# DLRM tower on one core: third block's root and second layer ahead of the last transfers and linear layer, squares summed on VectorE, bias products over 128 columns

## The reference

```python
e = stack([tbl_n[ids[:, n]] for n in range(26)], axis=1)      # 512 x 26 x 64
x = layer_norm(r_dense_t @ Wd.T, gd, bd)                      # 512 x 128
y = layer_norm(einsum('bnd,ed->bne', e, Ws), gs, bs)          # 512 x 26 x 128
y = layer_norm(einsum('bne,pn->bep', y, Wsi), gsi, bsi)       # 512 x 128 x 32
T = concatenate([x[:, None, :], swapaxes(y, 1, 2)], axis=1)   # 512 x 33 x 128
Z = einsum('bnd,bmd->bnm', T, T)
z = layer_norm(Z[:, TRIL_I, TRIL_J] @ Wl.T, gl, bl)[:, :384]  # layer norm over 512
h = maximum(concatenate([z, r_dense_t], axis=1) @ W_top1 + b_top1, 0)   # 512 x 512
h = maximum(h @ W_top2 + b_top2, 0)                           # 512 x 256
return h @ W_top3
```

## Time and profile before

| | us |
|---|---|
| median of 3 runs | 175.03 (173.59 to 177.0) |
| profiled execution, its own time | 173.57 |
| its span, first to last instruction | 171.8 |
| mean granted clock of TensorE | 0.98 |
| busy: PE, PEld, DVE, ACT, POOL | 143.2, 108.4, 129.6, 99.4, 101.1 |
| gathers, line 257: 104 instructions | 99.7 busy, 958 ns each |
| idle between gathers | 31.4 |

### The profile page before, as it was taken

One profiled execution on the slowest core, in us unless ns is written; L12 is line 12 of the kernel. 1 busy time (PEld: TensorE's weight loads), 2 busy tenths in 40 slices (PEclk: granted clock), 3 DMA queues, 4 the chain that ended last, 5 costly groups with the idle time before them and its releaser, 6 DMA issues.

```text
span 171.8 us, 4668 instructions
## 1 busy us (share of the span) xinstructions
PE 143.2 (83%) x1825; PEld 108.4 (63%) x1825; DVE 129.6 (75%) x300; ACT 99.4 (58%) x245; POOL 101.1 (59%) x111
## 2 busy tenths in 40 slices
PE   0179878798989946599999998969998899996995
PEld 0075543545559534467878685849695776886994
DVE  6359777796989498859899996949999877943151
ACT  0302344779765788667798686736676846721330
POOL 3777777777777777777777777777777200020000
PEclk9999999999999699879999999999999999999999
DMA  4833616133111113311111231111112200010000
GB/s 154 271 90 96 257 23 213 28 87 91 29 31 27 30 23 69 63 27 31 25 34 29 59 69 27 31 27 31 27 30 64 54 8 18 23 41 0 0 0 0
DMA packets 6003, 9.59 MB, mean 56 GB/s; under 512 B 2303, under 2 KB 3538, under 8 KB 5854
## 3 DMA queue, kind: packets, MB, share of 16 engines
q0 software_dynamic: 3392, 3.45, 11.0%
q1 hardware_dynamic: 2232, 5.08, 9.5%
q10 hardware_dynamic: 358, 0.78, 1.2%
HBM read 8.01 MB, written 0.00 MB: 47 GB/s over the span
## 4 chain that ended last, share of the span: by engine, by line
POOL 48%; PE 22%; issue 17%; DVE 5%; ACT 3%; DMA 2%; ACTq 1%; DVEq 0%
POOL g_sb L257 48%; PE psB L320 3%; PE psW L354 3%; PE psH L374 2%; PE psG L286 2%; PE psZ L335 1%; DMA g_sb<-in_table,row_id 1%; PE psZ L426 1%; PE psU L301 1%; PE psW L399 1%; DMA ids_sb<-in_ids 1%; ACT U L602 1%; ACTq L214 1%; DVE ssB L842 1%; DVE B L835 1%
## 5 line engine op out<-in xcount | busy, mean ns | idle before, releaser
L257 POOL DMA_INDIRECT g_sb<-in_table,row_id x104 | 99.7, 958 | 31.7 <-issue 31.4
L835 DVE TENSOR_TENSOR B<-psB,bias 128x512 f32<-128x512 f32 x31 | 20.0, 687 | 17.0 <-PE psB L320 16.9
L301 PE MATMUL psU<-wsi_x,g_sb 128*128 128x192 f32 (+4 forms) x128 | 21.3, 311 | 6.5 <-DVE g_sb L828 6.5
L301 PEld LDWEIGHTS psU<-wsi_x,g_sb 128*128 128x128 f32 x128 | 19.3, 193 | 10.1 <-DVE g_sb L828 10.1
L613 ACT ACTIVATE sqB<-B 128x512 f32<-128x512 f32 x31 | 19.1, 632 | 10.7 <-DVE B L835 10.5
L641 ACT ACTIVATE Zs<-psZ 32x264 f32<-32x264 f32 x59 | 22.3, 378 | 1.6 <-PE psZ L335 0.6
L320 PE MATMUL psB<-U,ws_g 64*128 64x512 f32 x64 | 19.9, 701 | 3.4 <-ACT U L602 3.3
L855 DVE TENSOR_TENSOR T<-B,psG 128x512 f32<-128x512 f32 x31 | 21.3, 687 | 1.1
L286 PEld LDWEIGHTS psG<-gram,sT 128*128 128x128 f32 x104 | 13.3, 197 | 13.7 <-ACT sT L589 10.8
L842 DVE TENSOR_REDUCE ssB<-sqB 128x16 f32<-128x512 f32 x32 | 21.7, 678 | 0.1
L286 PE MATMUL psG<-gram,sT 128*128 128x128 f32 x104 | 16.3, 297 | 0.7 <-ACT sT L589 0.7
(11 more groups left out here) (160 smaller groups left out, 217.2 us busy)
## 6 DMA issues: line engine op xcount, KB each, us to landing
g_sb<-in_table,row_id POOLq DMA_INDIRECT x104, 2.5
wl_sb<-in_wl SPq DMA_DIRECT2D x1, 1280.0 KB, 5.9
w_sb<-in_w SPq DMA_DIRECT2D x2, 512.0 KB, 5.4
w_sb<-in_w SPq DMA_DIRECT2D x1, 768.0 KB, 4.2
small_sb<-in_small SPq DMA_DIRECT2D x1, 615.5 KB, 3.7
dense_sb<-in_dense ACTq DMA_DIRECT2D x1, 512.0 KB, 7.2
Zt<-Zs SPq DMA_DIRECT2D x3, 80.0 KB
Zt<-Zs SPq DMA_DIRECT2D x3, 70.0 KB
```

The source lines that it names most:

```text
L257: pool.indirect_dma_start(g_sb[:, k, h * DSP:(h + 1) * DSP], None, table, bass.IndirectOffsetOnAxis(row_id[:, 2 * k + h:2 * k + h + 1], 0) ...
L301: mm = pe.matmul(psU[:, (lo - US * j) * PROJ:(hi - US * j) * PROJ], g_sb[:, SLOTS * b + c, :], wsi_x[:, c, lo - s0:hi - s0, :], start=(n = ...
L835: dve.tensor_tensor(B[:, h, :].rearrange("p (s j) -> p s j", j=PROJ), psB[h][:, :].rearrange("p (s j) -> p s j", j=PROJ), bias[:, :].rearr ...
```

## The change

1. ScalarE behind the steps: the third block's root (`deviation_w(LAST - 1)`) stands ahead of the relays. ScalarE issues one relay (q = 1) and GpSimd three (q = 2, 4, 6).
2. TensorE: `third_layer2(2, K1)` stands in front of the wait for the relays and in front of the whole linear layer of the last block, no longer behind its first quarter.
3. Last block: VectorE adds the four squares by three additions, and TensorE makes one product with ones where it made four. `top1(LAST, 1)` stands ahead of it. ScalarE's ReLU of the third block's second layer stands behind the last square.
4. `bias_part` takes its twelve products with the bias column repeated over 128 columns, six in step 4 and six in step 5; VectorE takes every 128th column of the bank at step 6. `shift_part` is spread over steps 1, 2 and 3 (1, 2 and 2 products), and VectorE takes its result at step 4.

```diff
-            for q in (2, 6):
+            for q in (2, 4, 6):
                 relay(pool, LAST, q, 1, 2, d_zt_pool)
...
             def last_block():
+                third_layer2(2, K1)
                 pe.wait_ge(d_zt[LAST], 10 * 16)
-                pe.wait_ge(d_zt_act, 2 * 16)
-                pe.wait_ge(d_zt_pool, 2 * 16)
+                pe.wait_ge(d_zt_act, 16)
+                pe.wait_ge(d_zt_pool, 3 * 16)
...
                 last_linear(0)
-                third_layer2(2, K1)
                 last_linear(1)
...
                 top1(LAST, 0, psF[0][:, 0:BS])
+                top1(LAST, 1, psF[0][:, BS:2 * BS]).then_inc(h1_f, 1)
                 pe.wait_ge(W_sd, LAST)
-                for f in range(FLIN // P):
-                    pe.wait_ge(sq_f, f + 1)
-                    mm = pe.matmul(psV[:, 0:BS], ones_sb[:, :], z_sq[:, f * BS:(f + 1) * BS], start=(f == 0),
-                                   stop=(f == FLIN // P - 1))
-                mm.then_inc(W_summed, 1)
-                top1(LAST, 1, psF[0][:, BS:2 * BS]).then_inc(h1_f, 1)
+                pe.wait_ge(sq_added, 3)
+                pe.matmul(psV[:, 0:BS], ones_sb[:, :], z_sq[:, 0:BS], start=True, stop=True).then_inc(W_summed, 1)
...
-            def bias_part():
-                pe.wait_ge(d_w1, 16)
-                pe.wait_ge(x1_ready, 1)
-                for f in range(K1):
+            def bias_part(lo, hi):
+                if lo == 0:
+                    pe.wait_ge(d_w1, 16)
+                    pe.wait_ge(x1_ready, 1)
+                for f in range(lo, hi):
                     for k in range(KZ):
-                        mm = pe.matmul(psH[:, f:f + 1], w1_sb[:, k, f * P:(f + 1) * P], bl_c[:, k:k + 1],
-                                       start=(k == 0), stop=(k == KZ - 1))
-                mm.then_inc(bz_done, 1)
+                        mm = pe.matmul(psH[:, f * P:(f + 1) * P], w1_sb[:, k, f * P:(f + 1) * P],
+                                       bl_c[:, k:k + 1].broadcast_to([P, P]), start=(k == 0), stop=(k == KZ - 1))
+                if hi == K1:
+                    mm.then_inc(bz_done, 1)
...
             keep_z(UNITS - 1, 1)
+            deviation_w(LAST - 1)
             act.wait_ge(Z_kept, 4 * UNITS)
-            for q in (1, 4):
-                relay(act, LAST, q, 1, 2, d_zt_act)
-            deviation_w(LAST - 1)
+            relay(act, LAST, 1, 1, 2, d_zt_act)
...
-            relu2(LAST - 1)
             act.wait_ge(W_f, 4)
             act.activation(z_sq[:, 3 * BS:4 * BS], psU[:, 0:BS], ACT.Square).then_inc(sq_f, 1)
+            relu2(LAST - 1)
             deviation_w(LAST)
...
                 dve.tensor_copy(zT[:, 2 * BS:3 * BS], psT[:, 0:BS]).then_inc(zT_f, 1)
+                for n, f in enumerate((1, 2, 3)):
+                    dve.wait_ge(sq_f, 1 + f)
+                    if n:
+                        dve.wait_ge(sq_added, n)
+                    dve.tensor_tensor(z_sq[:, 0:BS], z_sq[:, 0:BS], z_sq[:, f * BS:(f + 1) * BS],
+                                      ALU.add).then_inc(sq_added, 1)
                 dve.wait_ge(W_sd, BLOCKS)
```

More of the change, by code:

```diff
@@ L200, in tower @@
                              "y_copied"))
+        sq_added = sem("sq_added")
         W_f, zT_f, sq_f, hd_scaled, h1_f, h1a_f, h1T_f, h2_f = (
@@ L557, in step @@
                     x_sum()
-                    shift_part(0, 2)
+                    shift_part(0, 1)
                 if t == 2:
-                    shift_part(2, CW)
+                    shift_part(1, 3)
                 if t == 3:
-                    bias_part()
+                    shift_part(3, CW)
+                if t == 4:
+                    bias_part(0, 2)
+                if t == 5:
+                    bias_part(2, K1)
                 if late and j == 0:
@@ L1031, in step @@
                     third_zT(0)
-                if t == 3:
+                if t == 4:
                     dve.wait_ge(m_done, 1)
@@ L1039, in step @@
                                       ALU.mult).then_inc(m_shift, 1)
-                if t == 4:
+                if t == 6:
                     dve.wait_ge(bz_done, 1)
-                    dve.tensor_tensor(b1_z[:, :], psH[:, 0:K1], b1_c, ALU.add).then_inc(bz_ready, 1)
+                    dve.tensor_tensor(b1_z[:, :], psH[:, 0:K1 * P:P], b1_c, ALU.add).then_inc(bz_ready, 1)
                 if t < UNITS - 1:
```

## The result

The changed kernel takes 171.79 us (median of 20 executions, 170.96 to 173.35), the kernel before 173.78 (20 executions, 172.83 to 177.0). The ratio is 0.9884, with a 95% interval of 0.9855 to 0.9913: faster by 1.2%, or 2.0 us. The profiled execution has a span of 170.4 us where that of before had 171.8. The ratios leave out executions more than 1.5% above the fastest of their kernel, which for the kernel before are mostly those with a low clock of TensorE (0.95 to 0.97), so they say somewhat less than the clock is worth.

The account below looks back on a forecast made before the run. Gathers were taken to bound the kernel until 113 us, computation after. Root 1.26 + tail 0.64 + steps 0 = 1.9 us off the median gave 173.1, forecast as 173.0 us; own range 172.2 to 174.0, wide range 170.9 to 175.3.

Parts of the forecast that it names:

- What bounds the kernel: Gathers pace the kernel until 113 us, with at least 1.59 us of slack for computation; behind that, computation is the chain.
- The root: Behind the steps: third block's root starts at about 151.67 us instead of 153.33, ahead of ScalarE's transfers; gain 1.26 us.
- The transfers: Relays before the last linear layer: hidden, as TensorE asks at 156.88 us; rival that GpSimd's third sets the wait, chance 0.2.
- upper bound: Latest landing assumed for GpSimd's third relay, 156.7 us, hidden by only 0.2 us before TensorE asks.
- The tail: Behind the last linear block: one product with ones instead of four, second layer starts 3.57 us after it; gain 0.64 us.
- The steps: Steps 1 to 5: moved bias and shift products are covered by idle time and lie before the slack; gain 0.
- I count 0: Steps 1 to 5: removing one or both TensorE clock falls gains nothing, since both lie before the 1.59 us of slack.
- a rival at 1.7 us and 0.14: TensorE's clock falls count after all; fuller steps 4 and 5 remove one, gaining 1.7 us more, 171.4 us; chance 0.14.
- The sum: Whole kernel: 1.26 + 0.64 = 1.9 us off, 173.1 from the median, forecast as 173.0 us; chance 0.5 for 1.6 to 2.2.

Follow-up runs that it names:

- bias twice: Changed kernel with each of the twelve bias products in steps 4 and 5 done twice; ratio to the kernel before 0.9871, median 171.85 us.
- ones ahead: Changed kernel with second half of third block's second layer behind the first linear block, and the product with ones ahead of `top1(LAST, 1)`; ratio 0.9867, 171.87 us.
- the same with bias twice: The kernel of ones ahead with the bias products of steps 4 and 5 also done twice; ratio to the kernel before 0.9856, median 171.63 us.
- the narrow form: Kernel before with the edits of places in steps 1 to 5, but bias products kept in one-column form; ratio 1.0027, median 173.85 us.
- the single profile above: Profile of the changed kernel with second half of third block's second layer back behind the first linear block; ratio 0.9894, median 172.04 us.

## Why the prediction was right, and where it was not

**What bounds the kernel.** Right. Work in steps 4 and 5, in front of 113 us, was free (2.7 us of it), work behind it was not (0.88 us of 1.06), and A is 38.43 to 38.50 us in every profile in which the gather was waited for and unit 13 done once.

**The root.** Right, to 0.06 us at each point. Counted from the end of the sum of squares, and set on the clock of the first profile by taking off 0.41 us, the second layer's halves started at 154.50 and 155.74 (I had 154.44 and 155.72), the linear layer at 156.90 (156.88) and ended at 161.37 (161.36). The gain of this step is 1.25 us. What the prediction did not do is ask what the change's second edit costs by itself: its own sum has 0.12 us of waiting and 0.27 us of restart in it, and with the half left behind the linear block these would go. The run with it showed 0.29 us less.

**The transfers.** Right that they are hidden: no transfer held TensorE at 157.31, nor with the root ahead alone at 155.71, only 4.02 us behind the sum of squares. Wrong in the upper bound. I took the step between the first two landings, 1.4 us, for the third one. GpSimd's three landed 2.0 to 2.5 us after their starts (before, two: 2.1 and 3.0), the last one started at 153.3, so GpSimd's last landing was at 155.8 at the latest, which is 155.4 on the clock of the first profile, not 156.7. The Trainium skill's rule (DMA: Bandwidth & Descriptors, "Latency and other measured facts"), that a first byte takes longer from GpSimd's queue, can be neither seen nor excluded here: with the relay on either queue B was 16.45.

**The tail.** The step was mis-sized by a little. From the linear layer's end to the second layer's start it took 3.59 us (I had 3.57). But the second layer now starts from rest behind the ReLU, whose first product takes 0.49 us where the one at 166.83 took 0.42; 0.54 us remained of my 0.64. My remark that without `top1(LAST, 1)` ahead the additions would cost 0.33 us does not follow from my own times: they were to be done at L + 0.65, and `top1(LAST, 0)` ends at L + 0.67. The run with the product ahead did lose 0.34 us there, 0.12 of waiting and 0.22 of restart, so the figure came out by luck.

**The steps.** This is the part that failed, the term of the sum in "I count 0". The reading of the one profile was right: both falls in it lie ahead of slack and cost nothing. But by their mean clock other executions of the same kernel have three falls or more (0.97 and below in 50 of 66), so the profile at hand, with two, was one of the better ones. The edits in the steps lift the mean clock from 0.968 to 0.990, and alone they made the kernel 0.46% faster (0.17 to 0.75%), 0.8 us. I had this as a rival at 1.7 us and 0.14, and argued against it with the fact that the profile shows no fall behind 76 us. That was evidence of one execution only. The spread of the times before, 173.6 to 177.0, was the hint, and I named it and then let it go.

**The sum.** 1.9 was forecast; 1.80 us in the profiles, 2.0 (1.5 to 2.5) in the ratio. The parts don't add up without rest: 1.8 from the end and 0.8 from the steps are 2.6 us, a little above the interval. That the profile part and the steps' part are both right is possible within their intervals, since 0.8 has a lower end of 0.3. The forecast of 173.0 for the median was 1.2 too high, because the median of 175.03 on which it stood came from three executions, and twenty gave 173.78. The measured 171.79 lies inside the wide range, 170.9 to 175.3, but below the forecast's own, 172.2 to 174.0. That the ratio came out to the third digit (173.0 / 175.03 = 0.988) is in part luck: the measured one holds the 0.8 us of the steps that I had at nothing, against an end worth 0.1 us less than forecast, and its interval is 0.3% to either side.

**Open.** Why the steps' edits together lift the clock by 0.022, and whether each half lifts it at all, is not settled. The falls move from one execution to the next. One place comes back: eleven profiles have TensorE idle for 2.05 to 2.31 us near 80 us, for a gather, and in seven of them the clock falls inside that wait or within 2 us behind it; in the other four (changed, bias twice, ones ahead, the same with bias twice) it does not. The three that fell at 70 to 75 us waited 0.75 us or less near 80 and had no fall there. So that idle time goes with many falls but does not decide them alone. The page TensorE: Matmul & The Clock Gate of the Trainium skill, Part 1, says that the gate follows how busy the array has been; that busier steps 4 and 5 go with fewer falls agrees (0.990 against 0.968), though the narrow form moved there gave only 0.976. No profile of an execution with three falls was caught, so their price of about 1.0 us each rests on the times by clock, and its mechanism on the single profile above.

## What to carry to other kernels

Put the short instruction on which a chain hangs ahead of the transfers that share its queue: each issue took 0.8 to 0.9 us here and the root behind two of them came 1.7 us late. When a late input is placed in front of work that is ready, price the restart too (0.27 us for TensorE here), not only the wait. And count a clock fall over many executions, not in one profile: work ahead of slack is free until, as one profile showed here, two falls meet in front of the same slack.

## What was not expected of the hardware

The number of falls of TensorE's clock is a property of a single execution as much as of the kernel: the same program had mean clocks from 0.95 to 0.98. In the kernel before the times followed it by about 1.0 us for each 0.01, and in the changed kernel by 0.6 and 1.3 us for the two steps seen. One execution of the kernel before, out of 67, had a mean clock of 0.57 and took 235.31 us; it is left out above and unexplained.
